# A recommendation tower on one core: an earlier start of TensorE and of the table loads, seven instead of five early couples whose halves are added by DMA, gathers six groups ahead

## The reference, cut to what matters

```python
e = jnp.stack([tbl_0[ids[:, 0]], ..., tbl_39[ids[:, 39]]], axis=1)      # 512 x 40 x 64
vi = x[:, i_idx, :]; vj = x[:, j_idx, :]                                 # 780 pairs i < j
viW = jnp.einsum('bpd,pde->bpe', vi, W)
out = jnp.einsum('bpe,bpe->bp', viW, vj)                                 # z, 512 x 780
h = jnp.concatenate([z, dense_ctx], axis=1)
h = jnp.maximum(h @ W_top1 + b_top1, 0.0)                                # 512
h = jnp.maximum(h @ W_top2 + b_top2, 0.0)                                # 256
y = h @ W_top3
```

## Time and profile before

| | |
|---|---|
| median of 3 runs | 329.62 us (329.34 to 329.81) |
| the profiled execution's own time | 329.33 us |
| its span | 327.5 us |
| PE busy | 315.8 us (96%) |
| DVE busy | 258.3 us (79%) |
| POOL busy | 234.9 us (72%), and 34.7 us between its DMA issues |
| ACT busy | 219.4 us (67%) |
| chain that ended last | PE 73%, ACT 10%, DMA 8%, DVE 5% |

### The profile page before, as it was taken

The page is one execution under the profiler, slowest core; times in us unless marked ns, Lnnn a source line. Parts: engine busy times, 40 slices in busy tenths (PEclk is TensorE's granted clock), DMA queues, the critical chain, the costliest instruction groups (busy, mean ns, idle before and its releaser), DMA issues.

```text
span 327.5 us, 5637 instructions
## 1 busy us (share of the span) xinstructions
PE 315.8 (96%) x1488; PEld 111.6 (34%) x1488; DVE 258.3 (79%) x270; ACT 219.4 (67%) x1699; POOL 234.9 (72%) x196
## 2 busy tenths in 40 slices
PE   6999999999999999999999999999999999999996
PEld 1232343333323324333224333332233333234442
DVE  3798379778888898998999899989999987960000
ACT  3000220049984999699999999999999999810022
POOL 6787777777788767779879998999999773940000
PEclk9999999999999999999999999999999999999999
DMA  3555825242579799994333223223212200000000
GB/s 96 142 151 147 236 73 148 68 133 70 127 163 186 185 209 256 285 258 115 79 83 88 84 56 108 79 77 79 73 42 82 64 1 0 3 2 0 0 0 0
DMA packets 19320, 33.16 MB, mean 101 GB/s; under 512 B 4948, under 2 KB 5080, under 8 KB 19288
## 3 DMA queue, kind: packets, MB, share of 16 engines
q1 hardware_dynamic: 12344, 21.52, 22.1%
q0 software_dynamic: 5792, 9.71, 15.5%
q10 hardware_dynamic: 1152, 1.57, 1.7%
HBM read 22.82 MB, written 0.00 MB: 70 GB/s over the span
## 4 chain that ended last, share of the span: by engine, by line
PE 73%; ACT 10%; DMA 8%; DVE 5%; issue 3%; SPq 1%; DVEq 0%
PE ps_t L599 33%; PE ps_z L624 12%; PE ps_t L582 12%; ACT batched L416 9%; DMA prod<-in_tbl 8%; PE ps_t L633 6%; DVE prod L507 4%; PE ps_e L561 3%; PE ps_t L550 2%; PE ps_t L688 2%; PE ps_e L633 2%; DVE batched L521 1%; ACT E L400 1%; PE ps_e L570 1%; PE ps_t L666 0%
## 5 line engine op out<-in xcount | busy, mean ns | idle before, releaser
L416 ACT ACTIVATE batched<-batched 128x64 f32<-128x64 f32 x832 | 198.8, 253 | 0.0
L507 DVE TENSOR_TENSOR prod<-ps_t,E 128x1024 f32<-128x1024 f32 x148 | 171.0, 1217 | 16.6 <-PE ps_t L599 16.0
L416 ACT ACTIVATION_READ_ACCUMULATOR batched<-batched 128x1 f32 x832 | 165.9, 199 | 0.0
L369 POOL DMA_INDIRECT rows<-in_tbl,ids_sb x128 | 125.5, 981 | 35.1 <-issue 34.7
L599 PE MATMUL ps_t<-E,w_sb 64*128 64x512 f32 x592 | 145.3, 614 | 4.2 <-ACT E L400 2.0
L380 POOL TENSOR_TENSOR prod<-prod 128x1024 f32<-128x1024 f32 x38 | 89.9, 2373 | 13.2 <-DVE prod L507 12.7
L599 PEld LDWEIGHTS ps_t<-E,w_sb 64*128 64x128 f32 x592 | 51.1, 185 | 86.9 <-issue 57.0
L521 DVE TENSOR_TENSOR batched<-ps_t,wide_rows 128x1024 f32<-128x1024 f32 x52 | 60.1, 1218 | 7.9 <-PE ps_t L582 7.6
L582 PE MATMUL ps_t<-w_sb,E 64*128 64x512 f32 x208 | 48.4, 603 | 0.0
L624 PE MATMUL ps_z<-prod,quads 128*32 128x512 f32 x320 | 48.1, 602 | 0.0
L400 ACT ACTIVATE E<-ps_e 128x512 f32<-128x512 f32 x18 | 10.6, 591 | 49.2 <-PE ps_e L561 36.0
(11 more groups left out here) (43 smaller groups left out, 69.2 us busy)
## 6 DMA issues: line engine op xcount, KB each, us to landing
w_sb<-in_w_units SPq DMA_DIRECT2D x50, 256.0 KB, 2.7
prod<-prod POOLq DMA_DIRECT2D x10, 512.0 KB, 5.8
E<-E SPq DMA_DIRECT2D x48, 64.0 KB, 2.4
rows<-in_tbl,ids_sb POOLq DMA_INDIRECT x128, 3.3
w_sb<-in_w SPq DMA_DIRECT2D x7, 256.0 KB
E<-E ACTq DMA_DIRECT2D x24, 64.0 KB, 3.7
prod<-in_ids_by_field SPq DMA_DIRECT2D x2, 512.0 KB, 4.4
prod<-in_tbl SPq DMA_DIRECT2D x3, 312.5 KB
```

The costliest lines, as they stand in the source:

```text
L369: pool.indirect_dma_start(rows_of(u, b)[:, f * DIM:(f + 1) * DIM], None, tables[2 * k + f], bass.IndirectOffsetOnAxis(ap=ids_sb[:, col:col ...
L416: last = act.activation(products, products, ACT.Copy, accum_out=zt[:, b, at:at + 1])
L507: dve.tensor_tensor(prod[:, n % P_RING, s, :, :], ps_t[:, step % STEPS, :, :], multiplier, ALU.mult).then_inc(product_ready, 1)
```

## The change

Seven things are changed.

- SP issues the first table; ACT issues the second, as its first instruction. The broadcast ids and tables of the second couple still wait for both; those of the third are issued when the broadcast ids of the second have landed, not when its tables have. The first weights wait for all tables but the last.
- ACT's two copies of the spread ids are gone: DVE reads the spread ids from PSUM for the first couple's twenty codes.
- PE does three matmuls of the identity (128x128) with itself into `ps_z` before the spread; nobody reads them.
- Fields 6 are transposed one group earlier (before group 8 instead of behind it). The rest of the order is the same.
- Couples 3 and 5 (groups 6, 7, 10, 11) have their halves added by DMA: four more such DMAs of 512 KB, and eight matmuls (sixteen records) fewer in reduce_two.
- GATHER_LEAD is 6 instead of 7: each gather stands one group later in POOL's order.
- The broadcast ids are seen as int32 from the start (no instruction changes).

```diff
--- before.py
+++ after.py
@@ -36,7 +36,8 @@
 B_RING = 6
 STEPS = 3
 LAG = 7
-GATHER_LEAD = 7
+WARM_UP = 3
+GATHER_LEAD = 6
 PARAMS_AT = 12
 
 
@@ -81,7 +82,7 @@
 
 ADDED_COUPLES = (14, 15, 16, 18, 19, 20, 21, 23, 24, 25, 26, 27, 28, 30, 31, 32, 33, 34, 35)
 
-DMA_COUPLES = (7, 8, 10, 11, 13)
+DMA_COUPLES = (3, 5, 7, 8, 10, 11, 13)
 ADDED_BY_POOL = [n for n in range(NG) if n // 2 in ADDED_COUPLES]
 ADDED_BY_DMA = [n for n in range(NG) if n // 2 in DMA_COUPLES]
 ADDED = ADDED_BY_POOL + ADDED_BY_DMA
@@ -108,7 +109,7 @@
 
 
 def ahead(u):
-    return 0 if u in (6, 7) else 1 if u < 12 else 2
+    return 0 if u == 7 else 1 if u < 12 else 2
 
 
 SPLIT_FIRST = (0, 1, 3, 2)
@@ -202,7 +203,8 @@
             used, c = splits[f]
             small[f] = scratch[0:used, at:at + c * DIM].rearrange("p (c n) -> p c n", c=c)
             at += c * DIM
-        ids_wide = scratch[:, at:at + len(looked_up) * BATCH].rearrange("p (f n) -> p f n", f=len(looked_up))
+        ids_wide = scratch[:, at:at + len(looked_up) * BATCH].bitcast(I32).rearrange(
+            "p (f n) -> p f n", f=len(looked_up))
         at += len(looked_up) * BATCH
         codes = scratch[:, at:at + CODE_RING * BATCH].rearrange(
             "p (c n) -> p c n", c=CODE_RING)
@@ -239,7 +241,6 @@
         ids_first_cast = sem("ids_first_cast")
         pick_ready = sem("pick_ready")
         ids_spread = sem("ids_spread")
-        ids_spread_copied = sem("ids_spread_copied")
         small_loaded = {f: sem(f"small_loaded{f}") for f in looked_up}
         first_row_ready = sem("first_row_ready")
         first_row_cast = sem("first_row_cast")
@@ -308,16 +309,18 @@
         def _(sp):
             sp.dma_start(ids_first[:], ids_by_field[looked_up[0]:looked_up[0] + 2, :]).then_inc(ids_first_loaded, 16)
             sp.dma_start(ids_sb[:], ids).then_inc(ids_loaded, 16)
-            for u in range(LOOKED_UP):
-                if u > 0:
-                    for f in looked_up[2 * u - 2:2 * u]:
-                        sp.wait_ge(small_loaded[f], 16)
-                    sp.dma_start(ids_wide[:, 2 * u:2 * u + 2, :].bitcast(I32),
-                                 ids_by_field[None, looked_up[2 * u]:looked_up[2 * u] + 2, :].
-                                 to_broadcast([P, 2, BATCH])).then_inc(wide_loaded[u], 16)
+            def load_small(f):
+                sp.dma_start(small[f], tables[f].rearrange("(p c) n -> p c n", p=splits[f][0])).then_inc(small_loaded[f], 16)
+
+            load_small(looked_up[0])
+            for f in looked_up[0:2]:
+                sp.wait_ge(small_loaded[f], 16)
+            for u in range(1, LOOKED_UP):
+                sp.dma_start(ids_wide[:, 2 * u:2 * u + 2, :], ids_by_field[None, looked_up[2 * u]:looked_up[2 * u] + 2, :].
+                             to_broadcast([P, 2, BATCH])).then_inc(wide_loaded[u], 16)
                 for f in looked_up[2 * u:2 * u + 2]:
-                    sp.dma_start(small[f], tables[f].rearrange("(p c) n -> p c n", p=splits[f][0])).then_inc(
-                        small_loaded[f], 16)
+                    load_small(f)
+                sp.wait_ge(wide_loaded[u], 16)
 
             def load_params():
                 for c in range(ALL_CHUNKS):
@@ -333,7 +336,7 @@
                     sp.wait_ge(step_done, BLOCKS * (m - W_RING + 1))
                 sp.dma_start(w_sb[:, m % W_RING, :], w_units[m]).then_inc(w_loaded[m % W_RING], 16)
 
-            for f in looked_up:
+            for f in looked_up[:-1]:
                 sp.wait_ge(small_loaded[f], 16)
             for m in range(W_RING):
                 load_weights(m)
@@ -389,6 +392,9 @@
 
         @block.scalar
         def _(act):
+            f = looked_up[1]
+            act.dma_start(small[f], tables[f].rearrange("(p c) n -> p c n", p=splits[f][0])).then_inc(small_loaded[f], 16)
+
             def copy_fields(u):
                 if u < LOOKED_UP:
                     act.wait_ge(code_used, sum(len(codes_of) for codes_of in code_list[:u + 1]))
@@ -416,9 +422,6 @@
                     last = act.activation(products, products, ACT.Copy, accum_out=zt[:, b, at:at + 1])
                 last.then_inc(batched_summed, 1)
 
-            for i in range(2):
-                act.wait_ge(ids_spread, i + 1)
-                act.activation(ids_wide[:, i, :], ps_t[:, 0, i, :], ACT.Copy).then_inc(ids_spread_copied, 1)
             for u in SPLIT_FIRST:
                 copy_fields(u)
             left, time = [], 0
@@ -480,8 +483,8 @@
                         dve.wait_ge(code_used, j - CODE_RING + 1)
                     used, i = splits[f][0], looked_up.index(f)
                     if u == 0 and c == 0:
-                        dve.wait_ge(ids_spread_copied, i + 1)
-                    wide = ids_wide[0:used, i, :] if u == 0 else ids_wide[0:used, i, :].bitcast(I32)
+                        dve.wait_ge(ids_spread, i + 1)
+                    wide = ps_t[0:used, 0, i, :] if u == 0 else ids_wide[0:used, i, :]
                     dve.tensor_scalar(codes[0:used, j % CODE_RING, :], wide, float(c),
                                       first_row_f[0:used, i:i + 1], ALU.subtract, ALU.is_equal).then_inc(
                                           code_ready, 1)
@@ -635,6 +638,8 @@
                 return last
 
             pe.wait_ge(ident_ready, 1)
+            for _ in range(WARM_UP):
+                pe.matmul(ps_z[:, 0:P], ident[:], ident[:], start=True, stop=True)
             pe.wait_ge(pick_ready, 1)
             pe.wait_ge(ids_first_cast, 1)
             for i in range(2):
```

## The result

The changed kernel takes 339.62 us (median of four runs, 334.14 to 340.77), the one before 329.66 (329.34 to 329.81). It is 3% slower by these medians. The ratio given, 1.0216 with an interval of [1.0151, 1.028], leaves out runs more than 1.5% above a kernel's fastest, the profiled one among them, and rests on 334.14 and 339.13. It is slower clear of the noise; whether by 2% or more is open. The forecast was 326.0, faster. The profiled execution took 340.11, its span is 338.3.

A forecast was written before the change was run, and what follows sets the result against it. PE was taken to bound the kernel from 37 us, table loading before 29 us. Start 1.2, fields 6 0.7 and couples 1.7 made 3.6 us, below POOL's 4.2: 329.62 - 3.6 = 326.0 us, range 324.7 to 327.9.

The forecast's parts named there:

- POOL, the cover of all this: Check of POOL's gathers against PE's transpositions: PE can come forward 4.3 us at fields 11, 4.2 taken at fields 15.
- sign of being wrong: PE waiting 2 us ahead of the transpositions of fields 11 to 15, or first-couple codes below 0.5 us.
- A gather costs 1.25 us: POOL's time for each gather, 0.95 + 0.30 us, used to place all its later issues.
- Adds and lead: POOL before fields 11: five more DMA adds at 1.1 us, last gather issued at 96.52 + 5.5 = 102.0.
- 4.0 us to land: Time from a gather's issue to its landing, used at fields 11 and 15.
- Rival (3): POOL falls behind at fields 11, each new DMA add holding it longer; 332.5 us, chance 0.04.
- Rival (4): DMA adds compete with transfers in flight, weights or E4 late: no change; chance 0.06, split over no change and slower.
- fields 6 before group 8: PE's wait at group 9 for ACT's copy of fields 6 is hidden: gain 0.7 us, ends 0 and 0.7.
- couples 3 and 5: reduce_two on PE falls from 1.85 to 0.99 us for each: gain 1.7 us, ends 1.4 and 1.7.
- doubling of the rate: Possible effect of a second queue on the first tables: landed at 6.4 us, start gaining 3.8; not counted on.
- The start: Look-up before the first products: gain 1.2 us, ends -0.1 and 2.2, or 3.8 if the tables' rate doubles.
- my bounds: Time of one of DVE's codes from PSUM: 0.42 to 0.68 us, 0.62 taken.

The follow-up runs named there:

- the version in which POOL keeps up: Changed kernel with second table on SP, codes from SBUF, layer weights at fields 16, lead 7: 326.05 us; with five more identity matmuls 325.74 us.

## Why the prediction was wrong

The step that failed is "POOL, the cover of all this". It let PE come forward by 4.2 to 4.3 us, counting adds and lead as the only things that move POOL, and 4.0 us to land at every deadline. The last gather of fields 11 was to be issued at 102.0; it was issued at 111.24, and those of fields 13 took 8.4 us to land. PE's wait of 4.23 us is over the 2 us that the prediction named as its sign of being wrong. Term by term:

- *POOL's start*: taken as 3.33, unchanged; it was 6.20. I counted ACT's earlier issue as a gain for the tables and did not ask what was queued beside it. By the changed kernel with the table back on SP, 2.85 us, which buy no time once the long gather is gone (332.30 and 332.35).
- *A gather costs 1.25 us*: true except for one, at 10.26 + 0.30. I had priced the codes from PSUM on DVE and looked at PE alone. What they change is DVE's pace behind them: PSUM codes come later than PE wants them, so the next 24 have their buffers free and run without a pause. Before, DVE waited for PE between its codes, and these waits let POOL in. The Trainium skill, "SBUF — State Buffer", section "Who interferes with whom", says that tensor_scalar may run in a mode in which DVE and GpSimd lock each other out of a shared pair of ports, for a whole instruction, and that descriptor writing needs it. The trace agrees as far as it goes: gathers are 0.94 beside codes from PSUM and, when not shut out, 1.23 to 1.28 beside an unbroken run of codes from SBUF. That POOL stays out over more than one of DVE's instructions, here over some 24, is what the runs show.
- *Adds and lead*: +5.5 at fields 11 was right. With both start edits undone the last gather of fields 11 was issued at 102.0, the predicted figure. But these two were not free at fields 13. Seven couples instead of five move that gather from 126.01 to 128.77, and the time from 327.16 to 332.35.
- *4.0 us to land*: right at fields 11 (3.2 to 4.0 in four kernels), 8.1 to 10.6 at fields 13 in four with the layer weights at fields 12. I had called fields 11 the tightest and not checked fields 13: from issue to use they had 137.21 - 124.83 = 12.38 us before, less than the 13.75 at fields 11. With both start edits undone, 128.77 + 4.0 = 132.8 would have been in time, since PE came 4.1 us early, at 133.1; with 9.0 it was 4.64 late. The layer weights, the DMA adds and these gathers share full DMA engines there. No row of before shows the landing of fields 13's gathers, but the four DMA adds issued between 122 and 139 us took 9.9 us (median), not the 5.8 of all ten. Kernels with one edit between: 332.35 to 328.04 by moving the layer weights, to 326.05 by the lead, both with a part that is the varying start.
- *The price of a wait*: I had none for the clock. 4.7 us came on top of 8.5.

Rival (3), POOL falls behind at 332.5, had the right sign with a wrong mechanism, and named fields 11, where PE waits least (1.06): it wanted 1.95 us an add, and the adds cost what was predicted. Rival (4), competition in flight, was right in kind and sat on the gathers.

What held: fields 6 before group 8 took the wait at group 9 away (0.7); couples 3 and 5 are summed in 1.07 us (1.72 for couple 3, which fell into the half clock); the tables landed at 8.4 with no doubling of the rate. The start did not bring 1.2 but cost 0.3 (first products at 38.14 instead of 37.87): codes take 12.60 / 19 = 0.66 us, the upper half of my bounds, and the spread began 0.9 us later (3.62 instead of 2.73; the three identity matmuls alone end at 3.18, not 2.9), so the second couple began at 20.55 instead of 19.24. The Trainium skill, "VectorE: DVE Perf Modes", as cited in the prediction, had 0.66. (Two tables of 1250 rows are 0.640 MB, not 0.655, and 5.0 us; it changes nothing.) With ACT's copies and SP's table the start brought 1.4 (fields 3 at 31.37 against 32.81) where the pace doubled early. Overlap and early issue alone brought nothing: without the warm-up, and with a late doubling, fields 3 stood at 32.82. With 0.7 and 1.7 the 1.4 make 3.8, and the version in which POOL keeps up measures 3.2 to 3.7 less than before.

Two of the three losses on POOL cost nothing when put alone into the kernel before: the late ids (ratio 0.9981), and the codes from PSUM, without a long gather in the profiled execution (1.0004) or with one of 6.03 us (1.0001). The third, adds and lead, was not run alone there; with the other two undone it is not free (332.35 against 327.16 with five couples). In the changed kernel: the last gather of fields 3 is 2.5 us later than before, that of fields 4 another 8.4, 1.8 are made up till fields 7, and adds and lead take 5.7 up to fields 11, 14.7 in all. By the prediction's own count there were 13.75 - 4.0 = 9.75. That several edits draw on one account, each within its means, is what I missed.

What stays open: what decides whether POOL gets in between DVE's codes. Two gathers passed ahead of the long one in three kernels and none in two, at equal places in DVE's run one was shut out and one was not, and I have no rule for it. The stalled gather was 10.26, 10.13 and 4.85 us in three executions that share the codes from PSUM, the overlap and the warm-up, which may be why the changed kernel's own runs lie 6 us apart; no run tested it.

## What to carry to other kernels

An engine off the critical path is an account: write down its slack at each deadline and draw on it with all edits at once, its start, each instruction's stretch and the landing times at that very deadline. A change that removes an engine's waits can starve another that lived in these pauses. And a long wait of PE is to be priced with the slower clock behind it: 13.2 us for 8.5 of waits here.

## What the runs showed of the hardware

- Gathers issued beside an unbroken run of DVE's tensor_scalar on SBUF took 1.23 to 1.28 us each, or one of them took 4.85 to 10.26 us and ended within 1 us behind the run. Waits of DVE for its own last instruction (0.60 instead of 0.40 us each) kept them at 0.94.
- An 80 KB load took 1.9 us with no load on ACT's queue, and 4.8 with a 312 KB load of another queue issued 0.4 us ahead.
- Gathers landed in 2.8 to 5.1 us around 100 us in the kernel before. At fields 13 they took 8.1 to 10.6 us at a DMA share of 1.06 to 1.08, and 5.9 and 6.3 with the layer weights moved away (shares 0.91 and 0.85).
- PE's granted clock fell behind waits of 2.53, 2.69, 3.25, 3.96, 4.23, 4.64 and 5.51 us (a mean of 0.50 to 0.63 over the next 3.4 to 4.2 us, where 0.50 is the lower level), and stayed at 1.00 behind 1.06, 1.29, 1.44, 1.59 and one of 2.81: the wait's length alone does not decide it.
